# A decoder megakernel: the order of steps on every engine and the PSUM banks laid anew

## The reference: what is computed

```python
x = _layernorm(x + mamba(x))                 # L0 attn: in-projection, conv of 4 taps, scan over time
x = _layernorm(x + attention_map(x, ctx))    # L0 xattn
x = _layernorm(x + moe(x))                   # L0 ffn: 8 experts of 176, all computed, 2 weighted, shared 352
x = _layernorm(x + hgrn(x))                  # L1 attn: gated linear recurrence
x = _layernorm(x + topk_adjacency(ctx, x))   # L1 xattn: top 76 of 256 per row
x = _layernorm(x + moe(x))                   # L1 ffn: 8 experts of 128, shared 256
```

## Time and profile before

| | us |
|---|---|
| three runs | 615.7, 618.33, 619.99 |
| median | 618.33 |
| the profiled execution's span | 616.0 |
| PE busy | 523.1 (85%) |
| DVE busy | 498.5 (81%) |
| ACT busy | 428.5 (70%) |
| POOL busy | 266.5 (43%) |

### The profile page before, as it was taken

How to read it: one execution, slowest core, us unless ns; L and a number is a source line. 1 busy time by engine, 2 the same in 40 slices (tenths; PEclk the granted TensorE clock), 3 DMA queues, 4 the chain that set the end, 5 groups by cost and what they waited for, 6 DMA issues and landing times.

```text
span 616.0 us, 8787 instructions
## 1 busy us (share of the span) xinstructions
PE 523.1 (85%) x2416; PEld 372.7 (60%) x2416; DVE 498.5 (81%) x1133; ACT 428.5 (70%) x962; POOL 266.5 (43%) x418
## 2 busy tenths in 40 slices
PE   4956674898776899999889998899999899989856
PEld 3534453566653567767566677676776767767634
DVE  2089999998989999999986979999899996544332
ACT  2597579699968867897966986995798692332211
POOL 1088567346785522647432565564344421101110
PEclk9876587699979999999989999899999999999969
DMA  7295020382204460166005550560272047042000
GB/s 201 79 377 201 1 70 1 101 264 87 69 1 112 127 194 2 50 196 197 0 1 151 144 147 5 167 202 1 77 232 64 2 129 235 0 129 94 10 0 9
DMA packets 29823, 63.59 MB, mean 103 GB/s; under 512 B 4752, under 2 KB 8592, under 8 KB 29392
## 3 DMA queue, kind: packets, MB, share of 16 engines
q1 hardware_dynamic: 29776, 63.04, 33.3%
HBM read 61.91 MB, written 1.11 MB: 102 GB/s over the span
## 4 chain that ended last, share of the span: by engine, by line
PE 42%; DVE 26%; ACT 15%; issue 10%; POOL 3%; SPq 2%; DMA 1%; DVEq 0%; POOLq 0%; ACTq 0%
PE work L610 24%; PE work L667 9%; DVE acc L1187 5%; DVE st L1171 5%; ACT dA L962 5%; PE work L586 3%; PE h_bank L586 3%; DVE m L1136 2%; ACT L962 2%; DVE wk L1140 2%; ACT L831 2%; DVE h_tok L1089 2%; POOL dbu L548 2%; DVE du L1105 2%; DVE bst L1014 2%
## 5 line engine op out<-in xcount | busy, mean ns | idle before, releaser
L548 POOL TENSOR_TENSOR dbu<-du,b_rows 128x512 f32<-128x512 f32 x128 | 163.1, 1275 | 82.1 <-DVE st L1171 60.6
L962 ACT ACTIVATE dA<-dts,a_neg 128x127 f32<-128x127 f32 x512 | 156.9, 355 | 17.2 <-DVE st L1171 16.1
L1171 DVE TENSOR_TENSOR_SCAN st<-dA,dbu 128x512 f32<-128x512 f32 x128 | 155.1, 1214 | 6.4 <-ACT dA L962 6.1
L586 PE MATMUL h_bank<-ident,st 128*128 128x128 f32 x512 | 89.1, 305 | 41.2 <-DVE acc L1187 32.4
L610 PE MATMUL work<-stream,xsT 128*128 128x352 f32 (+1 forms) x320 | 111.1, 485 | 4.5 <-ACT xsT L831 1.9
L586 PEld LDWEIGHTS h_bank<-ident,st 128*128 128x128 f32 x512 | 66.3, 156 | 74.3 <-DVE st L1171 55.6
L1187 DVE SCALAR_TENSOR_TENSOR acc<-h_bank,c_cols,acc 128x512 f32<-128x512 f32 x128 | 92.9, 726 | 0.5 <-PE h_bank L586 0.4
L610 PEld LDWEIGHTS work<-stream,xsT 128*128 128x128 f32 x320 | 59.4, 200 | 33.8 <-issue 3.6
L493 POOL TENSOR_SCALAR var<-mv 128x1 f32<-128x1 f32 x56 | 12.7, 227 | 132.0 <-DVE mv L1015 131.1
L831 ACT ACTIVATE h_t<-work 128x384 f32<-128x384 f32 (+2 forms) x64 | 30.8, 482 | 37.6 <-PE work L586 37.5
L962 ACT ACT_TABLE_LOAD x43 | 55.2, 1283 | 0.8
(11 more groups left out here) (159 smaller groups left out, 824.4 us busy)
## 6 DMA issues: line engine op xcount, KB each, us to landing
stream<-in_stream SPq DMA_DIRECT2D x72, 352.0 KB, 3.5
stream<-in_stream SPq DMA_DIRECT2D x32, 384.0 KB, 3.7
b_rows<-b_dram SPq DMA_DIRECT2D x32, 256.0 KB, 4.4
stream<-in_stream SPq DMA_DIRECT2D x8, 360.0 KB, 3.7
stream<-in_stream SPq DMA_DIRECT2D x8, 256.0 KB, 2.7
wg<-in_wg SPq DMA_DIRECT2D x1, 1280.0 KB, 8.5
wu<-in_wu SPq DMA_DIRECT2D x1, 1280.0 KB, 11.0
wd<-in_wd SPq DMA_DIRECT2D x1, 1280.0 KB, 13.6
```

Source lines behind the costliest of these rows:

```text
L548: gp.tensor_tensor(tile, du[:, batch % 2, :, lo:hi], b_rows[:, b % 2, k:k + 1, :].to_broadcast([P, ET, P]), ALU.mult).then_inc(s["dbu_read ...
L586: return nc.tensor.transpose(dst, src, ident[:, :])
L962: last = A(dA[i % DA_RING][:, t, 1:P], dts[:, batch % 2, t, lo + 1:hi], ACT.Exp, scale=a_neg[:, t, k:k + 1])
L1171: V.tensor_tensor_scan(st[:, i % ST_RING].rearrange("p t l -> p (t l)"), dA[i % DA_RING].rearrange("p t l -> p (t l)"), dbu[:, i % DBU_RIN ...
```

## The change

- All four strings of `ORDER` and the string `BANK` are new. The chains, their steps and what a step issues are the same, so each engine has the same instructions in another order; only the compiler's table loads differ in number, since they depend on the order.
- SP gets a string of its own with seven more chains (`l` loads, `b` stores, `r` spreads, `c` chunks, `x`, `w`, `o`), so its transfers no longer follow PE's list. `x_loaded` becomes two semaphores, one for each buffer.
- Three waits are written out: PE's `adj` step 14 of batch 0 waits for the identity (part 3), DVE's `adj` step 14 of batch 2 and 3 waits for `row(5, ...)`, and DVE's `hgrn` step 6 waits for the read of `adjT`. The last two wait for earlier results of DVE itself.

```diff
@@ ORDER, two strings of many
     "pe": [
-        "ppp0ppppss00pppassssssaaaaaaaaaaaaasssssssssssss0ssp00sss00000spppssspsppsssss0000ss0ss0000s000000s0000s0s00s0",
+        "pppppppppsass0assssppsssssps0ssssssssss00s0ss00ss0spppsps0000s00000000s000s00s0ss0ss0000000sss00ppsss0000sss1p",
...
+    "sp": [
+        "lllcllblrrcblwrccccccccrccccccxcccccccccccbcrccccccccbccrcccwcwcoccccccccwocccccccccccccrccoccccccccccccrcwccc",
+        "ccocccccccccccccccoccwcccccccccccccoccccccoo",
+    ],
@@ sync engine
-            for stage, b, k in pe_order:
-                if (stage, k) == ("pre", 4):
-                    store_b(b)
...
+            for stage, i, k in sp_order:
+                if stage == "load":
+                    load_part(i)
+                if stage == "store":
+                    store_b(i)
+                if stage == "spread":
+                    spread_b(i)
+                if stage == "chunk":
+                    load_chunk(i)
...
+                if stage == "x":
+                    sp.wait_ge(*row(1, i - 2))
+                    sp.dma_start(x_rows[:, i % 2], d["x"][:, i, :]).then_inc(x_loaded[i % 2], 16)
@@ tensor engine, adj step 14
                     pe.wait_ge(s["adj_ready"], b + 1)
+                    if b == 0:
+                        pe.wait_ge(loaded[3], part_size[3])
@@ vector engine, adj step 14
                     dve.wait_ge(*full("adjT", b))
+                    if b >= 2:
+                        dve.wait_ge(*row(5, LT * (b - 1) - 1))
@@ vector engine, hgrn step 6
                     dve.wait_ge(*row(4, b))
+                    dve.wait_ge(*read("adjT", b // LT))
```

More of the change, by code:

```diff
@@ L88, in chains @@
         "1": [(stage, u, k) for u in range(U) for stage, k in layer1],
+        "l": [("load", part, 0) for part in range(7)],
+        "b": [("store", b, 0) for b in range(B)],
+        "r": [("spread", u, 0) for u in range(U)],
+        "c": [("chunk", i, 0) for i in range(U * 3 * F0.chunks)],
+        "x": [("xT", b, 0) for b in range(3, B)],
+        "w": [("x", u, 0) for u in range(2, U)],
+        "o": [("rows", u, 0) for u in range(U)],
     }
@@ L102 @@
     ],
     "dve": [
[L104 to L107, removed]
@@ L175, in decoder @@
 def decoder(nc, d, b_dram, out):
-    pe_order, dve_order, act_order, pool_order = (timeline(engine) for engine in ("pe", "dve", "act", "pool"))
+    pe_order, dve_order, act_order, pool_order, sp_order = (
+        timeline(engine) for engine in ("pe", "dve", "act", "pool", "sp"))
     with ExitStack() as ctx:
@@ L317, in decoder @@
         b_stored = [sem(f"b_stored{i}") for i in range(2)]
+        x_loaded = [sem(f"x_loaded{i}") for i in range(2)]
         stream_loaded = [sem(f"stream_loaded{i}") for i in range(STREAM_RING)]
@@ L412, in _, with load_part @@
         def _(sp):
-            def load_parts(parts):
+            def load_part(wanted):
                 for dst, src, part in loads:
-                    if part in parts:
+                    if part == wanted:
                         sp.dma_start(dst, src).then_inc(loaded[part], 16)
@@ L438, in load_chunk @@
             def load_chunk(i):
-                if i >= len(numbers):
-                    return
                 if i >= STREAM_RING:
@@ L481, in _ @@
-            store_rows(U - 1)
+            for stage, i, k in sp_order:
[7 more added lines that the diff above has]
+                    load_chunk(i)
+                if stage == "xT":
+                    sp.wait_ge(*full("gate", LT * (i - 2) - 1))
+                    sp.dma_start(xT[:, i % 3], d["xT"][:, :, i * L:(i + 1) * L]).then_inc(s["xT_loaded"], 16)
+                if stage == "x":
+                    sp.wait_ge(*row(1, i - 2))
+                    sp.dma_start(x_rows[:, i % 2], d["x"][:, i, :]).then_inc(x_loaded[i % 2], 16)
+                if stage == "rows":
+                    store_rows(i)
```

89 lines of the change are left out of this document (33 added, 56 removed).

## The result

The changed kernel takes 601.59 us, the median of four runs (600.59 to 603.29), against 617.02 us of four runs of the kernel before (614.09 to 619.99). The ratio is 0.975, with an interval of 0.971 to 0.979, so it is faster by 15.4 us. The forecast was 608.4 us. The time lies inside the range of 598 to 627 and the sign is right, but the gain is half as large again as the 9.9 us of the sum (by the profiled executions it is 616.0 to 601.4, 14.6 us).

What follows compares the result with a forecast made beforehand. DVE was taken to set the pace from the first scan to unit 3's FFN, then DVE and PE both. The terms -3.2 + 3.0 - 5.1 - 4.6 = -9.9 us took 616.0 to 606.1, plus 2.3 makes 608.4; range 598 to 627.

Steps and rivals of the forecast that it cites:

- What bounds the kernel: DVE sets the pace from 35.75 to 321.10 us (96% busy); to 507.10 PE and DVE are both nearly full.
- The start: Before the first scan: `hs` products start sooner and a convolution moves ahead, so DVE's idle time falls by 3.2 us.
- the 2.2 us allowed: Within the start: about ten `hs`-product records at the low clock, 0.22 us extra each, take 2.2 us back.
- The gate: Gate work and two table loads between the fifth and sixth `dA` make DVE wait: +3.0 us, between 0 and 5.4.
- Steps done when the scans end: More work done ahead by unit 3's FFN and the last scan shortens the end: -5.1 us, ends 0 and -7.7.
- Table loads: On ACT, 99 loads become 84, relieving it of 19.2 us; 24% of that gives -4.6 us.
- The share of the chain: Of all table loads' 109.1 us on L962 and L831, the chain holds 26.5 us, or 24%, taken as their price.
- The slower rival: Before unit 3's FFN, 30 us more of PE's busy time at 1.2 GHz adds 24 us: 632 us, chance 0.17.

Runs made afterwards that it cites:

- narrow products: POOL's wide products cut to a few columns, in both kernels: ratio 0.9892 (610.0 us) for the kernel before, 0.9633 (594.3 us) for the changed one.
- both cuts: Kernel before with POOL's wide products made narrow and every Silu, Exp, Ln and Tanh of ACT a Tanh: 598.41 us against 614.44, ratio 0.9724.

## Why the forecast was right in sign and short in size

**What bounds the kernel** was read rightly. DVE is the engine that sets the pace from the first scan to the last, and the whole gain lies in that stretch. The last scan's cut is at 492.2 us, forecast near 500, and PE's idle time from the first scan to there fell from 65.6 to 58.6, forecast 57.

**The start, -3.2: wrong.** These rows of the changed kernel's timeline answer to the earlier trace rows:

```profile
16.66 1.06 ACT L884 ACTIVATE hs<-du 128x1024 f32<-128x1024 f32 x1 [3.30 <-DVE du L1102]
...
17.86 6.79 PE L605 MATMUL work<-hs,w_x 128*128 128x256 f32 x16 [5.56 <-ACT hs L884]
...
24.58 1.99 PE L605 MATMUL work<-dt,w_dt 128*128 128x256 f32 x8
...
28.32 4.29 SPq L440 DMA_DIRECT2D b_rows<-b_dram  x8
...
34.16 1.55 POOL L543 TENSOR_TENSOR dbu<-du,b_rows 128x512 f32<-128x512 f32 x1 [20.93 <-DMA b_rows<-b_dram]
34.51 2.42 DVE L1102 SCALAR_TENSOR_TENSOR du<-work,cw,du 128x255 f32<-128x255 f32 x6
...
36.85 1.21 DVE L1170 TENSOR_TENSOR_SCAN st<-dA,dbu 128x512 f32<-128x512 f32 x1
```

The structure is the one forecast: the products start when `hs` is ready, and a convolution stands ahead of the first scan. But the low clock behind PE's pause of 5.56 us took more than the 2.2 us allowed: the 16 records take 6.79 us where they took 4.04, 2.75 more, with a granted clock of 0.54 from 17.86 to 24.58. All else at the start is 0.9 us later from the first load on, which is not the order's: PE's first product waits for its load until 6.89 us where it was 5.76, and over the traces of all orders that time lies anywhere between 5.75 and 7.13. `dt`'s products start 0.27 us sooner in place of 1.8. The other traces agree on the sign: with the tables loaded as usual, the first scan comes at 34.0 to 35.9 us with the old start and at 35.8 to 37.0 with the new one. DVE has done 9.96 us before the first scan (8.69), and its idle time there fell by 0.2 us in place of 3.2. POOL did come to wait for the spread of B, 20.93 us to 34.16, which the forecast named as what could take the gain back. But it did not hold the first scan: POOL's product is done at 35.71, ahead of the first `dA` (near 36.3, half of the eight exponentials that start at 35.13) and of the convolution that DVE is at from 34.51 to 36.93.

**The gate, +3.0: too dear.** The two loads stand where they were placed, and the one wait of DVE beside them is for the turn of the second state, which stands behind the gate in PE's list:

```profile
43.07 1.28 ACT L828 ACT_TABLE_LOAD   x1
...
44.36 0.60 ACT L828 ACTIVATE sg<-work 128x512 f32<-128x512 f32 x1
...
45.93 0.75 DVE L1186 SCALAR_TENSOR_TENSOR acc<-h_bank,c_cols,acc 128x512 f32<-128x512 f32 x1 [1.15 <-PE h_bank L581]
...
46.90 1.28 ACT L959 ACT_TABLE_LOAD   x1
```

DVE waits 1.15 us, and for PE's turn, not for `dA`: there is a convolution of 2.42 us in that place on DVE as well (at 41.23), which the term left out. With the gate put back the first group's last scan came 1.3 us sooner, but no gain in time could be told.

**Steps done when the scans end, -5.1: right on DVE, wrong on PE.** On DVE the counts hold. At unit 3's FFN the forecast had 6.7 us less done, and with narrow products it is 7.2 (270.34 to 263.18 us of DVE busy from the start). The forecast's 2.4 us ahead of the first scan and 3.5 behind the last are 2.3 and 3.2 in the ledger. On PE it had three products and two transposes, 4.2 us, done ahead by then, and so the time behind the last scan shorter by 4 us. It is 109.2 for 108.9. The last scan and the last state's transposes, before and then in the changed kernel:

```profile
505.38 1.22 DVE L1171 TENSOR_TENSOR_SCAN st<-dA,dbu 128x512 f32<-128x512 f32 x1
507.46 0.60 PE L586 MATMUL h_bank<-ident,st 128*128 128x128 f32 x4
...
490.45 1.22 DVE L1170 TENSOR_TENSOR_SCAN st<-dA,dbu 128x512 f32<-128x512 f32 x1
497.31 0.60 PE L581 MATMUL h_bank<-ident,st 128*128 128x128 f32 x4
```

The forecast took a place in PE's list for a place in time. Before, PE came to these transposes 0.9 us behind the scan's end; now it comes to them 5.6 us behind, so that the five steps ahead of them in its list are not done when the scans end. PE has 94.8 us of work left there, where it had 93.3.

**Table loads, -4.6: right in number, not measurable as a price.** The saved 20 us of ACT show in DVE's idle time as 0.4 us together with all else. The share of the chain, 24%, is no price of a load: by place it was 0.8 to 0.9 for each microsecond between two `dA`, and 0.03 to 0.06 on the average over all. That fewer loads kept the idle time from coming back fits the waits for `dA` with narrow products (5.1 us, against 11.4 in the old order), but no run tells it from the order itself.

**What was missing on the ledger, 10.2 us:** DVE's waiting for POOL. Every price in the sum was a mean from a row, and the mean of a row with that waiting in it hides it. L1021 stood in the page with one mean for 48 instructions, of which twelve took 0.64 to 1.50 us and the others 0.38 to 0.49. It is a missing entry and not the price of what was missing: with that waiting taken out of both orders, 16 us still lie between them. That the sign and the range were right owes something to luck: of the four terms the start brought nothing, the part of the steps that was to come behind the last scan did not come, and more than what they lacked came from something that the sum had no term for.

**The slower rival had the clock's sign wrong.** It asked what if more of PE's work fell to the 1.2 GHz level. The opposite came: the granted clock between the first and the last scan is 0.95 for 0.92, and about as many records (1926 and 1924, not all of them the same) take 396.7 us in place of 405.8. Over the whole run the same 2416 records take 511.4 us in place of 523.1. In the first group's scans the clock was 0.61 and is 0.79, with more of PE's work in them:

```profile
35.75:63.50 27.75, 16.73 (x64) 11.15 (x64) 27.24 (x31) 21.54 (x69) 25.80 (x38) 0.61 0.67 268
36.85:70.80 33.95, 24.85 (x100) 15.36 (x100) 31.12 (x43) 27.84 (x80) 25.18 (x38) 0.79 0.45 174
```

**What stays open** is how the 15.4 us divide. On DVE's ledger they are 10.2 of waiting and 5.4 of moved work. But a kernel before that is spared the waiting alone keeps 7 of 20 us, so in the new order its other limits, `dA` and PE, must be eased along with it; fewer loads and PE's higher clock are what could do that, and no run shows that they do. DVE's idle time is the same 30 us in both orders, but not the same waits: for `h_bank` ahead of `acc` DVE waits 7.8 us where it waited 0.5. How much each of these brought can't be read from cuts that hide each other; the changed kernel with both cuts, which would give the distance without POOL and without loads, wasn't run. Nor is it shown why PE's clock is higher in the new order.

## What to carry to other kernels

Keep a ledger of the engine that sets the pace, between two events that both kernels have: busy time, instructions, idle time; when the same instructions take a different busy time, look at the longest of a row and not at its mean. Where DVE and POOL both work on SBUF, put the two-input products of POOL beside scans with an operand in PSUM, PSUM additions or maxima, and not beside normalizations. A place ahead in an engine's list is a place ahead in time only if the engine gets there in time. And a cut that brings little doesn't show that the thing cut is free: cut its neighbour as well before you cross it off.

## What the hardware showed that I had not expected

- A TENSOR_SCALAR or SCALAR_TENSOR_TENSOR of DVE with all its tensors in SBUF that meets a POOL product of 1.27 us is booked as a longer instruction: 0.88 us more for each product of POOL, and up to 1.50 us in the kernel for one that can take 0.38. MAX8 and the statistics, also from SBUF, are not. POOL's products keep their mean of 1274 to 1277 ns.
- 98 table loads less, 126 us of ACT's time, brought 3.3 us in the old order, and eight loads more (with 1.6 us of activations) cost 9.4.
- The same 2416 matmul records took 523.1 us in one order and 511.4 in the other; between the first and the last scan the granted clock was 0.92 and 0.95.
